# Narrow attention: query stores by SyncE in later steps, the context on a semaphore of its own, the slopes cast by ScalarE

## The reference, cut to what matters

```
# x: 8 x 256 x 128, ctx: 8 x 512 x 128
# layer two: slopes and positions as a bias, one is added to the softmax sum
Q, K, V = split_heads(norm(x) @ Wq.T), split_heads(ctx @ Wk.T), split_heads(ctx @ Wv.T)   # 8 x 16 x (256 or 512) x 8
scores = Q @ K^T * 8**-0.5 - slope[h] * (query_pos - key_pos)        # then -inf where mask == 0
e = exp(scores - max(scores));  attn = e / (1 + sum(e))
x = x + tanh(g) * ((attn @ V) @ Wo.T)
# layer three: biases on Q, K, V and the output, scale 128**-0.5, causal and padding mask, plain softmax
# layer one, second part: int8 rounding of norm(x) and of a 128 x 128 matrix, product, rescale
```

## Time and profile before

| | |
|---|---|
| median of 3 runs | 1514.68 us (1513.16 to 1520.35) |
| profiled execution, its own time | 1525.43 us |
| its span in the trace | 1523.7 us |
| PE busy, share of the span | 87% |
| DVE, ACT, POOL busy | 66%, 53%, 50% |

### The profile page before, as it was taken

The page is one execution under the profiler, slowest core; times in us unless marked ns, Lnnn a source line. Parts: engine busy times, 40 slices in busy tenths (PEclk is TensorE's granted clock), DMA queues, the critical chain, the costliest instruction groups (busy, mean ns, idle before and its releaser), DMA issues. The chain is left out here.

```text
span 1523.7 us, 33033 instructions
## 1 busy us (share of the span) xinstructions
PE 1329.0 (87%) x11864; PEld 747.8 (49%) x11872; DVE 1000.3 (66%) x3093; ACT 807.3 (53%) x1190; POOL 763.1 (50%) x727
## 2 busy tenths in 40 slices
PE   5999968827999999999845799999899957999994
PEld 4444454713666666666642344344567723444432
DVE  4988844156766676667475577676455776777766
ACT  3777723335655565656421666567443214666664
POOL 4776613522766676667726445352150057665631
PEclk9999988966999999999955799999799976999997
DMA  4566635436324431440036344330220034233200
GB/s 149 195 226 227 235 125 174 122 128 247 130 82 153 153 132 63 152 153 1 2 51 179 93 114 100 101 86 4 57 46 1 1 72 110 55 62 72 55 6 29
DMA packets 93965, 157.80 MB, mean 104 GB/s; under 512 B 18409, under 2 KB 63620, under 8 KB 90223
## 3 DMA queue, kind: packets, MB, share of 16 engines
q1 hardware_dynamic: 76456, 121.47, 26.7%
q10 hardware_dynamic: 12480, 30.29, 5.5%
q0 software_dynamic: 4880, 4.04, 1.3%
HBM read 99.16 MB, written 50.62 MB: 98 GB/s over the span
## 5 line engine op out<-in xcount | busy, mean ns | idle before, releaser
L2105 DVE CUSTOM_DVE_ANT_0 a_junk<-a_psM,a_madd 128x512 bf16<-128x512 f32 x480 | 313.2, 686 | 109.9 <-issue 105.5
L2048 ACT ACTIVATE a_probs<-a_psE 128x1024 f32<-128x1024 f32 x256 | 262.0, 1024 | 124.0 <-PE a_psE L1908 123.0
L2492 DVE TENSOR_REDUCE a_mx<-a_psM 128x1 f32<-128x512 f32 x236 | 148.2, 669 | 124.5 <-PE a_psM L2316 124.5
L2453 ACT ACTIVATE a_probs<-a_psE 128x1024 f32<-128x1024 f32 x128 | 130.9, 1025 | 85.6 <-PE a_psE L2338 82.3
L2286 POOL TENSOR_TENSOR a_half_sum<-a_probs 128x1024 f32<-128x1024 f32 x64 | 150.9, 2358 | 32.7 <-ACT a_probs L2453 32.7
L1920 PE MATMUL a_psO<-a_probs,narrow_values 128*32 128x256 f32 x2048 | 163.9, 394 | 1.8 <-ACT a_probs L2048 1.1
L1874 PE MATMUL a_psM<-narrow_k_op,narrow_q_op 57*64 57x512 bf16 (+1 forms) x960 | 146.5, 405 | 18.2 <-DMA a_cT<-in_ctxT 10.3
L2334 PE MATMUL a_psE<-a_qT,a_kT 64*128 64x256 f32 x1024 | 133.9, 381 | 0.0
L2350 PE MATMUL a_psO<-a_probs,a_values 128*64 128x256 f32 x1024 | 124.6, 385 | 0.8 <-ACT a_o_raw L2437 0.8
L2474 DVE RECIPROCAL a_o_raw<-a_o_raw 128x256 f32<-128x256 f32 x64 | 111.4, 1741 | 11.0 <-ACT a_o_raw L2437 11.0
L1898 PE MATMUL a_psE<-narrow_q_op,narrow_k_op 60*64 60x256 bf16 (+1 forms) x2048 | 109.4, 287 | 6.6 <-DMA narrow_q_op<-a_max_parts 5.8
(11 more groups left out here) (396 smaller groups left out, 2735.7 us busy)
## 6 DMA issues: line engine op xcount, KB each, us to landing
wide_k<-a_k_stage SPq DMA_DIRECT2D x32, 512.0 KB, 2.6
a_k_part<-wide_k SPq DMA_DIRECT2D x64, 256.0 KB, 3.6
wide_v<-a_v_stage SPq DMA_DIRECT2D x24, 512.0 KB, 3.9
a_kT<-wide_k ACTq DMA_DIRECT2D x6, 2048.0 KB
a_values<-wide_v ACTq DMA_DIRECT2D x6, 2048.0 KB
keys<-a_parts SPq DMA_DIRECT2D x96, 64.0 KB
narrow_k_op<-keys SPq DMA_DIRECT2D x30, 192.0 KB
narrow_q_op<-a_queries SPq DMA_DIRECT2D x28, 192.0 KB
```

The costliest lines, as they stand in the source:

```text
L2048: act.activation(probs[:, head:head + 2, k:k + 2, :], psE[es % 2][:], ACT.Exp).then_inc(exped, 1)
L2105: dve.tensor_tensor_reduce(junk[j][:], max_bank(s, j, first), madd[r][:, t, :], 1.0, -3.0e38, ALU.add, ALU.max, mx[r][:, max_place(h, t):m ...
L2453: act.activation(probs[p % 2][:, :, 2 * half:2 * half + 2, :], psE[half][:], ACT.Exp).then_inc(exped, 1)
L2492: dve.tensor_reduce(mx[r][:, at:at + 1], max_bank(2 * p + t, j, first), AX.X, ALU.max).then_inc(max_read, 1)
```

## The change

Three edits. SP takes over the stores of query pieces 1 to 3 from ACT: piece 1 is stored ahead of the first `cross_masks`, pieces 2 and 3 in steps 0 and 1, behind `cross_masks(v + 1)` and ahead of the second half's maximum rows. POOL cuts pieces 2 and 3 in steps 0 and 1 too, behind `turned_masks(v + 1)`. The context tile counts on its own semaphore, for which PE waits in slot 11. The slopes are cast by ACT, behind its first rounding.

```
@@ class NarrowConstants, gpsimd
-        pool.tensor_copy(self.slopes_b[:], self.slopes[:]).then_inc(self.slopes_cut, 1)
+
+    def scalar(self, act):
+        act.wait_ge(self.const_in, 32)
+        act.copy(self.slopes_b[:], self.slopes[:]).then_inc(self.slopes_cut, 1)
@@ narrow_attention
-        n_loads = n_keys + 2 + 1
-        n_first = 2 * N_COPIES + 1
+        n_loads = n_keys + 2
+        n_first = 2 * N_COPIES
-        loaded = [ph.sem(f"loaded{i}") for i in range(RING)]
+        loaded, context_in = ([ph.sem(f"{n}{i}") for i in range(RING)] for n in ("loaded", "context_in"))
@@ SyncE
                 def load_context(u):
-                    sp.dma_start(cT[u % RING][:], ...).then_inc(loaded[u % RING], 16)
+                    sp.dma_start(cT[u % RING][:], ...).then_inc(context_in[u % RING], 16)
...
                 load_queries(1)
+                sp.wait_ge(split, 4)
+                store_queries(sp, 1)
                 cross_masks(0)
...
                     if v + 1 < B:
                         cross_masks(v + 1)
+                    if v + 2 < NCHUNK:
+                        sp.wait_ge(split, 4 * (v + 2))
+                        store_queries(sp, v + 2)
                     maxima(v, 1)
@@ GpSimd
                 own_masks(0)
-                for n in range(1, NCHUNK):
-                    split_queries(n)
+                split_queries(1)
                 turned_masks(0)
                 own_masks(1)
                 for v in range(B):
                     split_max(v, 0)
                     if v + 1 < B:
                         turned_masks(v + 1)
+                    if v + 2 < NCHUNK:
+                        split_queries(v + 2)
@@ TensorE, slot V_SLOT
                                 pe.wait_ge(max_negated, 2 * v + 1)
+                                pe.wait_ge(context_in[r], 16 * (turn + 1))
@@ ScalarE
-                for n in range(1, NCHUNK):
-                    act.wait_ge(split, 4 * n)
-                    store_queries(act, n)
@@ layer1_int8, ScalarE
                 rounding(0)
+                ahead.scalar(act)
                 rounding(1)
```

More of the change, by code:

```diff
@@ L1688, in load_context @@
                 def load_context(u):
-                    sp.dma_start(cT[u % RING][:], io["ctxT"][:, u * S2:(u + 1) * S2]).then_inc(loaded[u % RING], 16)
+                    sp.dma_start(cT[u % RING][:], io["ctxT"][:, u * S2:(u + 1) * S2]).then_inc(context_in[u % RING], 16)
                 def load_queries(u):
```

## The result

| | before | after |
|---|---|---|
| median of the runs beside each other | 1517.51 us (1513.16 to 1520.81, 4 runs) | 1498.16 us (1496.17 to 1500.95, 4 runs) |
| ratio of after to before | | 0.9876, 95% interval 0.9838 to 0.9913 |
| profiled execution; its span | 1525.43; 1523.7 us | 1500.08; 1498.2 us |

The change makes the kernel faster, by 18.8 us or 1.2%, as the ratio has it (the interval: 13 to 25 us). The forecast was 1498.1, or 16.6 us less. That the time itself is met to a tenth is luck: the runs of before beside these have a median 2.8 us above the one that I had started from. The gain holds as a sum, but not by its terms: layer three gave less than forecast, the clock cost nothing, and the slopes brought something.

The account below looks back on a forecast made before the run. ACT's stalls in issuing query stores at both narrow layers' starts were taken as the bound. The terms 11.3 + 7.3 - 2.0 = 16.6 us, off 1514.68, gave 1498.1 us; 8 in 10 range 1489 to 1508.

Parts of the forecast that it names:

- The bound: Starts of both narrow attention layers: ACT's waits end last, 24.1 us in layer two and 19.7 us in layer three.
- Score 0 of layer two, 16.2 us sooner: Batch 0's first score in layer two: without stores on ACT it comes at 835.2 instead of 851.39.
- Then the path of before repeats: Layer two, POOL's first operation on the maxima to score 0: 5.1 us as before, plus 0.9 for SP.
- Score 8 of layer two, 11.3 us sooner: Layer two, batch 0: mask, cut and SP's stores make PE wait 4.9 us, so 11.3 of 16.2 us are left.
- The clock, -2.0: TensorE behind score 8 of layer two: the new 4.9 us wait leaves the clock low, costing 2 us.
- Layer three, 8.0 and 7.3 us sooner: Layer three, batch 0: score 0 comes 8.0 us sooner, set by POOL, and score 8 7.3 us sooner.
- The context, nothing: PE's wait ahead of its first product: PE and DVE begin at most 4.3 us sooner, but score 0 gains nothing.
- The slopes, nothing: Int8 block: POOL's 3.78 us cast goes to ACT's idle time of 5.48 us; no gain.
- the queue, mild: Second-half rows behind SP's stores land 4.1 us later in both layers; 14 us given back, 1512; chance 0.13.
- Nothing new waits: Stores issue quickly, mask lands in 4.7 us, clock high; nearly all of 16.2 + 8.0 kept, 1490.5 us; chance 0.11.
- The queue, hard: SP held by its own stores, second-half rows land after 11.8 us; 27 us lost, some 1542; chance 0.04.
- half: Masks come later because SP's loads are slower; score 0 moves by only half, 1506 us; chance 0.10.

Follow-up runs that it names:

- e1: Kernel before with only the stores' part: SP stores later query pieces, POOL's cuts moved with them; ratio to before 0.9909.
- e10: e6 with the loads of batch 1's keys, positions, context and queries moved behind the first maximum rows; only run 1510.59 us.
- e6: Kernel after, but SP issues batch 0's first-half maximum rows ahead of piece 1's six stores; ratio to before 0.987.
- e4: Kernel after, but POOL cuts pieces 1, 2 and 3 all ahead of the turned mask, as before; ratio to before 0.9921.
- e9: e6 with the load of batch 1's turned mask moved behind the first maximum rows; ratio to before 0.9881.
- e12: e11 with the 15 loads for batch 1 issued by ACT instead of SP; ratio to before 0.9875.
- e5: Kernel after, but ACT issues piece 1's six stores behind its first negation of the maxima; ratio to before 0.9909.
- e7: e6 with piece n stored behind step n - 1's first rows, pieces 2 and 3 cut later, batch 1's turned mask loaded ahead of mask copies; ratio to before 0.9925.
- e8: Kernel after, but the context counts on the same semaphore as keys and queries again; ratio to before 0.9871.
- e2: Kernel before with only the slopes cast by ACT instead of POOL; ratio to before 0.9988, int8 block 26.9 us.
- e3: Kernel before, but POOL casts the slopes twice; int8 block 32.9 us against 29.8 before.
- e11: e9 with piece 1 stored behind batch 2's mask loads, pieces 2 and 3 cut and stored a step later; ratio to before 0.9869.

## Why the prediction was right, step by step

- **The bound** (ACT's stalls in issue, on the path): right. Both waits are gone and both first scores came sooner (e1). One reading was loose: of ACT's 24.1 us in layer two 20.75 were issue, and the rest was the wait for POOL's cut of piece 1, which ended at 818.44.
- **Score 0 of layer two, 16.2 us sooner:** 10.8 measured. POOL's part held to 0.5 us. What failed is the step "Then the path of before repeats", with 5.1 us and 0.9 for SP from POOL's first operation on the maxima to score 0. It took 10.85 (819.53 to 830.38): SP came to the rows only at 823.89, their issue took 3.07 us instead of 2.14, and they landed 3.4 us behind it instead of 1.3. The 5.1 us were read at a moment when the DMA engines idled. With the loads for batch 1 and piece 1's stores out of the way the same step gives +28.5 (e10). SP's six stores took 6.6 us, not 4.5; e6 shows that this alone cost nothing, since score 0 stays at +35 without them.
- **Score 8 of layer two, 11.3 us sooner:** 10.1 measured, but not by my reason. The delay fell on score 0 and the wait forecast at score 8, 4.9 us, shrank to 0.6. The turned mask landed 6.5 us behind its issue (6 taken).
- **The clock, -2.0:** not paid. The granted clock rose at about 834.6 (0.84 on average in 834 to 836), 4.3 us behind score 0 as in before, and there was no long wait at score 8. Behind score 8 it was 1.00, the 2.4 GHz level:

```profile
844.00:846.00 2.00, 2.00 (x38) 0.69 (x30) 1.30 (x6) 1.19 (x2) 0.46 (x1) 1.00 0.84 135
```

- **Layer three, 8.0 and 7.3 us sooner:** 5.5 and 5.8 measured. For this layer I had counted six stores ahead of the second rows only, but piece 1's stand ahead of the first; with them out of the way score 0 gains 8.0 (e6). By the end of the program 3.7 are left. 1.7 go in one place, step 4, where the eight scores between 64 and 72 took 15.1 us in before and 16.8 in after. The same stretch took 15.1 us in e4 and e9 to e12, 15.4 in e6, 16.6 to 16.7 in e5, e7 and e8, and 18.2 in e1. With one trace of each kernel a variation between executions can't be told from an effect of the order; its cause stays open.
- **Step 1, nothing:** right within a us: PE's wait for the first rows is 1.3 us there, 0.6 before, and it has none for the second.
- **The context, nothing:** right (e8).
- **The slopes, nothing:** wrong, by 2.8 us to the good side. ACT's side held (the cast took 3.60 us, and the next rounding came 5.96 us behind the first, 6.20 before). The failed step is "POOL idled behind it anyway": I asked who waited for POOL, not what ran beside it (e2, e3).
- **The sum:** by the traces 10.5 + 1.0 + 3.7 + 2.8 = 18.0 against 16.6. Layer three gave 3.6 less than its 7.3, layer two 0.8 less than its 11.3; the clock gave 2.0 more, the slopes 2.8, the experts 1.0. So the closeness is in part luck.
- **The rivals:** *the queue, mild* had the right mechanism at the wrong place, at the first rows and for 2.1 (3.4 - 1.3) and 2.9 us. *Nothing new waits* would have needed idle DMA engines. *The queue, hard* did not come, nor did *half*: score 0 of layer two moved by two thirds, and not for slow masks.

## What to carry to other kernels

When a stall is removed, look at what was being worked off in its shade: the DMA engines' share over the same microseconds tells whether the next wait is already there, and a landing time read while they idled holds only while they idle. Order small DMAs that an engine waits for ahead of bulk, and don't expect much of another issuing engine (1.3 us of 7.9 here). An operation on an idle POOL isn't free while DVE is on the path: compare DVE's durations beside it with the same operations elsewhere.

## What the runs showed of the hardware that I had not expected

- Beside POOL's casts DVE's operations are held up: a 128x512 fp32 operation took 3.70 us instead of 0.43, a group of four 4.38 instead of 1.11 (e3). The Trainium skill ("SBUF — State Buffer", Who interferes with whom) has DVE, in a mode that uses both its ports, and GpSimd share a port pair as an exclusive lock: whoever comes first holds it for the whole instruction. By that rule an operation of DVE that meets one of POOL's ends just behind it, and the trace agrees (0.3 us behind the cast of 3.59, 0.9 behind that of 3.67); in which mode DVE ran, the profile doesn't show.
- DMAs of 2 KB landed 1.3 us behind the end of SP's issue with the queues light (e10, DMA share 0.02), and 1.8 (e7, layer three) to 7.9 us (e11, layer two) with stores or loads in flight, from their own queue or another's.
- The issue itself slows: in after six stores of 128 KB took SP 6.62 us while loads were in flight (1.1 each; DMA share 1.00 in 811 to 817 and 0.71 in 817 to 823), 3.41 later (0.57 each; 0.03 in 836 to 838), and 8.04 in e12 behind three masks.
